# Axial attention: keys kept without padding, and the two products of a step issued on opposite halves of the array's rows

## The reference, cut to what matters

```python
q = (x @ Wq).reshape(b, n, 32, 16)            # b = 8, n = 256, DIM = 512
k, v = jnp.split(ctx @ Wkv, 2, axis=-1)       # ctx has 256 columns
q, k = apply_axial_rope(q, pos_map), apply_axial_rope(k, ctx_pos_map)
logits = jnp.einsum('bqhd,bkhd->bhqk', q, k) * scale
w = jax.nn.softmax(logits, axis=-1)
attn = jnp.einsum('bhqk,bkhd->bqhd', w, v)
x = _layernorm(x + attn.reshape(b, n, 512) @ Wout + bout)
```

## Time and profile before

| | |
|---|---|
| median of three runs | 2910.94 us (2908.63 to 2911.35) |
| the profiled execution | 2908.72 us, its span 2906.9 us |
| mean granted TensorE clock | 0.951 |
| PE busy over the span | 2467.0 us (85%) |
| DVE | 1799.7 us (62%) |
| ACT | 1248.9 us (43%) |
| the axial stage | first maximum product at 2023.1 us, last operation at 2619.5 us |

### The profile page before, as it was taken

How to read it: one execution, slowest core, us unless ns; L and a number is a source line. 1 busy time by engine, 2 the same in 40 slices (tenths; PEclk the granted TensorE clock), 3 DMA queues, 4 the chain that set the end, 5 groups by cost and what they waited for, 6 DMA issues and landing times. The chain is left out here.

```text
span 2906.9 us, 42566 instructions
## 1 busy us (share of the span) xinstructions
PE 2467.0 (85%) x15730; PEld 1904.7 (66%) x15746; DVE 1799.7 (62%) x5199; ACT 1248.9 (43%) x2982; POOL 297.7 (10%) x535
## 2 busy tenths in 40 slices
PE   5889999999974999799999999995888888883674
PEld 4668999998864999476667766763655555551332
DVE  6656767667875666445445544454566666657986
ACT  3434445444433211244344434452544444436663
POOL 3211100001000000000000000002111111101220
PEclk8999999999986999999999999997999999996887
DMA  4101211112005000000000000001000000003001
GB/s 156 62 23 41 70 37 40 69 36 74 29 26 194 1 1 1 1 1 1 1 1 1 1 1 1 1 1 51 5 5 5 5 5 5 5 1 133 1 1 58
DMA packets 41212, 83.41 MB, mean 29 GB/s; under 512 B 4528, under 2 KB 17840, under 8 KB 39856
## 3 DMA queue, kind: packets, MB, share of 16 engines
q1 hardware_dynamic: 41008, 80.70, 7.9%
HBM read 72.30 MB, written 8.39 MB: 28 GB/s over the span
## 5 line engine op out<-in xcount | busy, mean ns | idle before, releaser
L1990 DVE TENSOR_REDUCE s_nmax<-s_a_ps 128x2 f32<-128x512 f32 x256 | 174.3, 686 | 198.7 <-PE s_a_ps L1772 195.7
L651 ACT ACTIVATE s_p<-s_ms,s_nmax 128x256 f32<-128x256 f32 x256 | 128.5, 503 | 192.3 <-DVE s_nmax L754 192.3
L754 DVE CUSTOM_DVE_ANT_0 s_ms<-s_s_ps,s_bias 128x256 f32<-128x256 f32 x256 | 98.2, 421 | 175.9 <-PE s_s_ps L529 175.5
L1375 ACT ACTIVATE l_wo_w<-l_wo_w,s_nmax 128x128 f32<-128x128 f32 (+1 forms) x256 | 114.4, 447 | 197.8 <-DVE s_nmax L1471 197.0
L512 PE MATMUL s_q_ps<-s_xT,s_wh 128*128 128x256 f32 x1024 | 189.6, 286 | 0.0
L1215 PE MATMUL s_s_ps<-l_wqb_w,s_lT 128*128 128x512 f32 x384 | 175.7, 597 | 16.0 <-DVE l_wo_w L1441 15.3
L914 PE MATMUL s_h_ps<-s_xh,s_t 128*128 128x256 f32 x704 | 173.0, 284 | 9.3 <-DVE s_xl L1002 9.3
L1886 ACT ACTIVATE s_pT<-s_s_ps 128x512 f32<-128x512 f32 x256 | 151.6, 606 | 59.6 <-PE s_s_ps L1785 57.3
L562 PE MATMUL s_y_ps<-s_wh,s_oT 128*128 128x512 f32 x512 | 173.0, 399 | 0.0
L914 PE MATMUL s_h_ps<-s_xl,s_t 128*128 128x256 f32 x704 | 172.4, 283 | 0.0
L512 PEld LDWEIGHTS s_q_ps<-s_xT,s_wh 128*128 128x128 f32 x1024 | 165.5, 193 | 6.0 <-issue 0.5
(11 more groups left out here) (304 smaller groups left out, 6686.8 us busy)
## 6 DMA issues: line engine op xcount, KB each, us to landing
s_x_raw<-kept SPq DMA_DIRECT2D x24, 512.0 KB, 3.3
s_c_in<-in_ctx_T SPq DMA_DIRECT2D x32, 256.0 KB, 2.5
l_wqb_w<-in_l_xwq SPq DMA_DIRECT2D x4, 1024.0 KB, 7.8
l_wqb_w<-in_l_xwo SPq DMA_DIRECT2D x4, 1024.0 KB, 10.1
kept<-s_x_raw SPq DMA_DIRECT2D x8, 512.0 KB, 2.7
l_wo_w<-in_l_wo SPq DMA_DIRECT2D x1, 4096.0 KB, 15.5
s_raw<-in_l_w1T SPq DMA_DIRECT2D x2, 2048.0 KB, 9.9
s_raw<-in_l_w2T SPq DMA_DIRECT2D x2, 2048.0 KB, 21.5
```

Of the source, the lines that this page charges most:

```text
L651: act.activation(p[:, h % PR, q, :], ms[:, h % 2, q, :], ACT.Exp, scale=-1.0, bias=nmax[:, h % PR, q:q + 1], accum_out=den[:, h % PR, q:q ...
L754: dve.tensor_tensor_reduce(ms[:, h % 2, q, :], s_ps[:, h % 2, q * S:(q + 1) * S], bias[:, h // PER % B, :], -SCALE, 3.0e38, ALU.add, ALU.m ...
L1375: act.activation(p[:, h % PR, q, 0:(q + 1) * P], ms[:, h % 2, q, 0:(q + 1) * P], ACT.Exp, scale=-1.0, bias=nmax[:, h % PR, q:q + 1], accum ...
L1990: dve.tensor_reduce(nmax[:, g % 2, :, 2 * pair + e], a_ps[:, n % 2, :].rearrange("p (q k) -> p q k", q=QT), AX_X, ALU.max, negate=True).th ...
```

## The change

Keys are stored without padding: kT holds two heads on 128 partitions. Neighbouring heads now lie on opposite halves of a tile (`head_of`), and as LAG is odd, heads n and n-11 do too. One function `products(n, j)` issues the four matmuls of a step alternately, maximum, score, maximum, score, each over 64 rows, the two of a pair on opposite halves and in different banks. Both waits, of the maximum and of the score product, now stand ahead of all four, and the transposes of the step behind them.

The outputs come once in eight steps (PV_LAG = 21, step 5 modulo 8) for all eight heads of a group, so pT holds sixteen heads. Their reciprocal follows in the next step (OUT_LAG = 22). The projections' steps are others. The padding's zeros and one of the two ACT operations of a "k" transpose are gone. The semaphore counts of pv_done and fixed follow.

```diff
     LAG = GH + 3
-    QUADS = H // 4
-    QUAD_LAG = LAG + 3 + 2
-    OUT_LAG = QUAD_LAG + 5
-    Q_AT, K_AT, V_AT, Y_AT = (10, 14), (19, 21), (12, 13), (16, 18)
+    PV_LAG = LAG + GH + 2
+    OUT_LAG = PV_LAG + 1
+    Q_AT, K_AT, V_AT, Y_AT = (8, 11), (19, 21), (15, 16), (18, 20)
     def head_of(n):
-        return n // GH, n % 4, n % GH // 4
+        return n // GH, n % GH // 2, n % 2
...
-        kTz = m.sb("kTz", [P, H, S], F32R)
+        kT = m.sb("kT", [P, H // 2, S], F32R)
-        pT = m.sb("pT", [P, GH, QT, S])
+        pT = m.sb("pT", [P, 2 * GH, QT, S])
...
-            def greatest(b, n):
+            def greatest_wait(b, n):
...
                 pe.wait_ge(a_out, b * H + n + 1)
-                for q in range(QT):
-                    mm = pe.matmul(a_ps[:, n % 2, q * S:(q + 1) * S], qTx[:, g % 2, pair, q * P:(q + 1) * P],
-                                   kTz[:, GH * g + 2 * pair + e, :], start=True, stop=True)
-                mm.then_inc(a_full, 1)
-            def scores(b, whose, n):
+            def scores_wait(b, whose, n):
...
                 pe.wait_ge(s_out, (b + shift[whose]) * H + n + 1)
-                for k in range(QT):
-                    mm = pe.matmul(s_ps[:, n % 2, k * S:(k + 1) * S], kTz[:, GH * g + 2 * pair + e, k * P:(k + 1) * P],
-                                   qTm[:, g % 2, pair, :], start=True, stop=True)
-                mm.then_inc(s_full, 1)
-            def outputs(b, m):
-                g, e = m // 2, m % 2
-                pe.wait_ge(s_out, b * H + 2 + 4 * m + 4)
-                if e == 0:
-                    pe.wait_ge(o_out, b * G + g + 1)
...
+            def products(n, j):
+                for part in range(QT):
+                    if n is not None:
+                        g, pair, e = head_of(n)
+                        rows = slice(XD * e, XD * (e + 1))
+                        mm = pe.matmul(a_ps[:, n % 2, part * S:(part + 1) * S], qTx[rows, g % 2, pair, part * P:(part + 1) * P],
+                                       kT[rows, PAIRS * g + pair, :], start=True, stop=True)
+                        if part == QT - 1:
+                            mm.then_inc(a_full, 1)
+                    if j is not None:
+                        g, pair, e = head_of(j)
+                        rows = slice(XD * e, XD * (e + 1))
+                        mm = pe.matmul(s_ps[:, j % 2, part * S:(part + 1) * S], kT[rows, PAIRS * g + pair, part * P:(part + 1) * P],
+                                       qTm[rows, g % 2, pair, :], start=True, stop=True)
+                        if part == QT - 1:
+                            mm.then_inc(s_full, 1)
+            def outputs(b, g):
+                pe.wait_ge(s_out, b * H + 2 + GH * (g + 1))
+                pe.wait_ge(o_out, b * G + g + 1)
+                for e in range(2):
+                    for k in range(QT):
...
+                                               pT[:, GH * (g % 2) + 2 * pair + e, k, :],
...
                 mm.then_inc(pv_done, 1)
             def steps_of(b):
                 for n in range(H):
+                    whose = "prev" if n < LAG else "here"
+                    if has(b, whose):
+                        scores_wait(b, whose, (n - LAG) % H)
                     if has(b, "here"):
-                        greatest(b, n)
+                        greatest_wait(b, n)
+                    products(n if has(b, "here") else None, (n - LAG) % H if has(b, whose) else None)
                     for use in t_turns.steps[n]:
...
-                    whose = "prev" if n < LAG else "here"
-                    if has(b, whose):
-                        scores(b, whose, (n - LAG) % H)
-                    whose = "prev" if n < QUAD_LAG else "here"
-                    if n % 4 == QUAD_LAG % 4 and has(b, whose):
+                    whose = "prev" if n < PV_LAG else "here"
+                    if n % GH == PV_LAG % GH and has(b, whose):
...
-            act.copy(kTz[0:XD, 1::2, :], blank[0:XD, :]...).then_inc(fixed, 1)
-            dve.tensor_copy(kTz[XD:P, 0::2, :], blank[XD:P, :]...).then_inc(fixed, 1)
...
-                    heads = slice(GH * g, GH * (g + 1), 2)
-                    act.copy(kTz[0:XD, heads, cols], t[0:XD])
-                    heads = slice(GH * g + 1, GH * (g + 1), 2)
-                    act.copy(kTz[XD:P, heads, cols], t[XD:P]).then_inc(t_out, 1)
+                    act.copy(kT[:, PAIRS * g:PAIRS * (g + 1), cols], t).then_inc(t_out, 1)
```

More of the change, by code:

```diff
@@ new lines, in outputs @@
+            def outputs(b, g):
[3 more added lines that the diff above has]
+                    for k in range(QT):
+                        for part in range(2):
+                            for pair in range(PAIRS):
+                                ones_or_values = one[:, e, :] if part else v[:, k, GH * g + 2 * pair + e, :]
+                                mm = pe.matmul(o_ps[32 * pair:32 * pair + 32, part, :], ones_or_values,
+                                               pT[:, GH * (g % 2) + 2 * pair + e, k, :],
+                                               start=(e == 0 and k == 0 and part == 0),
+                                               stop=(e == 1 and k == QT - 1 and part == 1))
@@ L1815, in steps_of @@
                             rows_over(b + shift[use[0]], t_turns.at(b, use), t_turns.bank(b, use), *use[1:])
-                    whose = "prev" if n < LAG else "here"
-                    if has(b, whose):
-                        scores(b, whose, (n - LAG) % H)
-                    whose = "prev" if n < QUAD_LAG else "here"
-                    if n % 4 == QUAD_LAG % 4 and has(b, whose):
-                        if whose == "here" and n == QUAD_LAG:
+                    whose = "prev" if n < PV_LAG else "here"
+                    if n % GH == PV_LAG % GH and has(b, whose):
+                        if whose == "here" and n == PV_LAG:
                             pe.wait_ge(f_out, f_turns.at(b, ("here", "v", QT - 1)) + 2)
-                        outputs(b + shift[whose], (n - QUAD_LAG) % H // 4)
+                        outputs(b + shift[whose], (n - PV_LAG) % H // GH)
                     for use in f_turns.steps[n]:
@@ L1854, in _ @@
                            ACT.Sin).then_inc(sines, 1)
-            act.wait_ge(fixed, 1)
-            act.copy(kTz[0:XD, 1::2, :], blank[0:XD, :].unsqueeze(1).broadcast_to([XD, H // 2, S])).then_inc(fixed, 1)
             def rows_over(at, bank, of, g, q):
@@ L1899, in _ @@
                 rows_over(q, q % 2, "x", 0, q)
-            act.wait_ge(fixed, 4)
+            act.wait_ge(fixed, 2)
             for n in range(2 * QT):
@@ L1934, in _ @@
             dve.wait_ge(sines, 1)
-            dve.wait_ge(fixed, 1)
-            dve.tensor_copy(kTz[XD:P, 0::2, :], blank[XD:P, :].unsqueeze(1).broadcast_to([XD, H // 2, S])).then_inc(fixed, 1)
             for t in range(2):
```

14 lines of the change are left out of this document (7 added, 7 removed).

## The result

The changed kernel takes 3008.74 us, the median of four runs (3007.21 to 3018.66), against 2911.14 (2908.63 to 2919.92) for the kernel before, run beside it: a ratio of 1.0337 with a 95% interval of 1.0306 to 1.0368. Slower was right; the time lies above the range of 2922 to 2998. The profiled execution is the slowest of the four, 3018.66 us with a span of 3016.9, and 10 us above their median; so what is read from its trace is somewhat larger than in a usual execution.

A forecast was written before the change was run, and what follows sets the result against it. PE and DVE take turns waiting; no engine fills the stretch. Per middle element +6.2 us from placement and +1.2 from clock: 6 x 7.4 + 8 = 52 on 2908.7 gives 2961, median 2963, range 2922 to 2998.

The forecast's parts named there:

- Side by side: Products on opposite row halves overlap: 0.12 us a pair, a head 0.24 for 0.48, at best 7.7 us less per element.
- Shape changes: Switching between 64-row products and 128-row work costs 0.18 us on each side; a step with a transpose takes 0.97, before 0.85.
- Rival 2: No price for switching between half and whole rows: a step with a transpose takes 0.61 us, total 2935; chance 0.2.
- rival 1: No overlap on row halves: each head on PE's path costs 0.24 us more, total 2994; chance 0.2.
- The waits moved together: Step 3 (modulo 8) waits for the "m" transposes of steps 1 and 2: 0.7 us idle, four times an element.
- the walk: Step-by-step timing of one element's 32 steps in four windows: 16.5 + 19.9 + 44.5 = 80.9 us, against 74.7 before.
- The pieces placed anew: Values, projections and normalisation at their new steps, over one element: 80.9 us against 74.7, +6.2.
- Theory C: A rival posed after the result: the moved pieces alone cost more than the walk says; no chance given.
- The clock: Values of step 29 run at clock 0.50 in every element: +1.7 us against about 0.5 now, so +1.2.
- the other waits bring it too: Upper case of the clock term, low clock from PE's other waits as well: up to about 5 us.
- At the ends: First and last element, lacking normalisation or next projections, take half the loss each: 8 us together.
- Rival 3: PE was the bound and gets shorter: 8.9 us less per element, total 2840, or 2875 with half spent; chance 0.15.

The follow-up runs named there:

- e11: The changed kernel with LAG 12 in place of 11, both products on the same half, values one step later: 3044.52 us, ratio 1.0447.
- e3: The kernel before with packed keys and products over 64 rows, every piece at its old place: 2967.79 us, ratio 1.0186.
- e7: The changed kernel with LAG 13 in place of 11, giving the "m" transposes two more steps before the scores: 3009.13 us, ratio 1.0332.
- e13: The changed kernel with 26 idle weight products per element on PE, written to the transpose bank used next: 2982.14 us, ratio 1.0244.
- e6: The changed kernel with a group's values in two halves, at steps 4 and 0 modulo 8, projections shifted to fit: 2965.63 us, ratio 1.0176.
- e1: The changed kernel with both maximum products issued before both score products: 3011.66 us, ratio 1.0335.
- e2: The changed kernel's order of work, but padded keys and products over 128 rows one after the other, pT holding twelve heads: 2987.59 us, ratio 1.0253.
- e12: The kernel before with DVE's product that finishes a group's outputs moved ahead of the rotation in step 22 and v's copy in step 14: 2914.69 us, ratio 1.0001.
- e4: The changed kernel with 26 idle weight products per element on PE, written to the values' output bank: 3039.69 us, ratio 1.0434.
- e9: The changed kernel with idle weight products in steps 25 to 28 only (1, 3, 1, 6), written to the values' output bank: 3020.78 us, ratio 1.0367.

## Why the prediction was right in its sign and wrong in its size

*Side by side, 0.24 for a head in place of 0.48.* Right that they run at once: starts 0.00 to 0.01 apart, and 0.23 lost in a step of e11. But the second pair comes 0.22 behind the first, not 0.12.

*Shape changes, 2 x 0.18, and a step of 0.97.* The step takes 0.90, so the two changes and the slower second pair cost 0.29 together in place of 0.36. Right in kind, and a little too dear. Rival 2 (0.61) is refuted by this, rival 1 (PE's takings in turn) by the starts. e3 shows the price directly, 2.2 us over eight steps at full clock.

*The waits moved together, 0.7 four times.* The size is right: PE's wait for the "m" transposes is 0.67 to 0.74. The count is not: PE has 13 such waits in 6.6 elements, two in each, at steps 3 and 11. In step 19 the y projection of step 18 covers it and in step 27 DVE is later, as the walk itself had it. Taking the wait away gained nothing in e7, where another took its place in step 3; what it alone is worth isn't shown.

*The pieces placed anew.* Right. Without half clock (e13) the walk's 80.9 us measure 82.1, the idle products' own cost included; each window is within 0.6 us. In the changed kernel PE waits 1.8 us before the second v projection (1.9 expected) and 1.7 before the second y (1.6). That the values in one piece are part of it, e6 shows. Theory C falls.

*The clock, 1.7 us in the values of step 29, +1.2 net.* This is the first of two terms that failed, by its size. The place was right: step 29 has 3.3 to 6.6 us at half clock in every element and takes 6.5 us in the element shown, 4.5 in e13. But the prediction looked for the low clock in one piece of one step, and it holds for 24 us of the element: steps 25 to 29 and 2 to 4 throughout, and the values of step 5 and the projection of step 20 in some elements. The term is 3.7 to 5.4 us in place of 1.2, close to or above the bound of about 5 set for the case that "the other waits bring it too", which is what happened. By itself this would have left the time in the range: 2963 + 6 x 4.2 = 2988 at most. 87.50 = 80.9 by the walk + 1.2 by which e13 exceeds it + 5.4.

*At the ends, 8 us.* The second term that failed, and in a usual execution the larger miss. The first element takes 71.5 us from its first maximum to the next element's, 56.1 before, and the last one 73.9 from its first maximum to its last, 58.2 before; with 3.5 behind them that is some 34 us. Here the views by stretch of the first element, before and after:

```profile
2023.90:2079.96 56.06, 50.03 (x376) 35.01 (x379) 36.32 (x72) 30.75 (x55) 15.89 (x42) 0.95 0.02 6
```

```profile
2023.50:2094.97 71.47, 60.02 (x368) 34.99 (x367) 36.17 (x72) 26.48 (x47) 17.15 (x46) 0.78 0.01 5
```

Half clock rose from 5.9 to 30.9 us in the first element and from 2.3 to 34.1 in the last, but the clock can't be all of it: in e13 the last one has 6.8 us of it and still takes 67.9. The prediction took half a middle element's loss for each; each loses more than a whole one, 15.4 and 15.8 us against 12.6. What the other kernels lose at the ends narrows it (here the ends are the time from the stage's first maximum product to the first matmul of the next stage, less six periods; 173.6 us before):

| kernel | period, us | half clock per element, us | ends above before, us |
|---|---|---|---|
| the change | 87.50 | 23.9 | 34 |
| e1, other order of issue | 85.87 | 21.6 | 33 |
| e2, new order, whole rows | 84.97 | 15.9 | 17 |
| e3, old order, half rows | 81.67 | 14.0 | 18 |
| e6, half rows, values in halves | 82.29 | 14.7 | 13 |
| e7, LAG 13 | 88.12 | 29.6 | 24 |
| e13, idle work | 82.14 | 0.6 | 35 |

Whole rows or values in halves take half of the loss or more away, and idle work, placed for the middle elements, none. How the 26 us missing there divide into clock and waits stays open.

The sum: on the profiled execution, which is 3018.7 us where 2961 was forecast, 6 x (12.62 - 7.4) = 31 us are missing in the middle elements and 26 at the ends, 57 together. That execution is 10 us above the median, and the forecast had put the median 2 above it. For a usual execution e1 stands in, as an estimate: 6 x (85.87 - 74.88 - 7.4) = 22 us in the middle and 33 - 8 = 25 at the ends, 47 together, where the medians differ by 3008.7 - 2963 = 46. Of the 22, some 15 are the clock, 6 x (3.7 - 1.2), and 7 the walk's shortfall of 1.2 an element. So in a usual execution about half of the miss is at the ends, a third is the clock of the middle elements, and either of the two alone would have left the time in the range.

*Rival 3, PE was the bound.* Refuted: the time rose, and DVE's waits for the maximum product grew from 33% to 44% of the stretch.

What lowers the clock is shown only in part. The order alone does it (e2, 15.9 us), 9.1 of it in the window from step 25 on; that it is so because PE waits there behind DVE's normalisation with no values left to do is a reading of the timeline, where PE waits 2.98 us before step 29. Products over 64 rows alone do it too, with every piece in its place (e3, 14.0 us against 1.9); the change has both and 23.9. Why half rows bring the clock down these runs don't show. In e6, e3 and e2 nearly the same time at half clock goes with totals 22 us apart, so the time at half clock isn't by itself the loss: it costs where PE is the one waited for.

## What to carry to other kernels

Where two engines take turns, a gain on one is paid out only at the places where the other waits for it; follow the chain of the other engine (here DVE's normalisation) across the whole stretch before a shortened product or a removed wait is counted: e12's low clock taken away gained nothing, and e7's removed wait was followed by another. A rearrangement that lets TensorE wait longer had a second price here, its clock: put it on every stretch where TensorE waits, not on the one piece that showed it before, and let the range reach to that. The first and the last round of a loop, which lack the work of their neighbours, deserve a walk of their own; half of the miss lay there. To size a clock term afterwards, give the waiting engine idle work in a bank that is free by then; idle work in a bank that another engine must empty first measures that wait instead (e4, e9).

## What the hardware did that was not expected

- Matmuls on opposite row halves start together also when the program issues both of the one half first, then both of the other (e1: starts 2300.63 and 2300.63, then 2300.85 and 2300.86; the third in the program starts before the second). The order in the source is no means of keeping them apart; the same half is (e11).
- Products over 64 rows, every piece of work at its old step, raised the time at half clock from 1.9 to 14.0 us per element and slowed the kernel by a ratio of 1.0186 (1.0166 to 1.0207) (e3).
- Adding 11 us of idle matmuls to each element made the program 27 us faster (e13 against the change; medians of runs on two chips, each with its own runs of before: ratios 1.0244 and 1.0337).
- After a change of shape the second matmul comes 0.22 us behind the first, and only the following ones at 0.12 (e11: 2301.04, 2301.26, 2301.38, 2301.50). In a step of two pairs that first distance is the only one there is.
